# A decoder layer on one core: the expert bias matmul reads 128 rows instead of 24

## The reference, cut to what matters

```python
x = _layernorm(x + _L0_attn_ref(x, ...))             # 16 heads of 8, one shared k and v head
x = _layernorm(x + _L0_xattn_ref(x, ctx_512, ...))   # causal self part plus cross part on 512 rows
x = _layernorm(x + _L0_ffn_ref(x, Wg, W1, b1, Wo, bo))

def _L0_ffn_ref(x, Wg, W1, b1, Wo, bo):              # D = 128, H = 256, E = 8, top 2
    gate_scores = softmax(einsum('btd,ed->bte', x, Wg))
    topk_val, topk_idx = top_k(gate_scores, 2)
    comb = (one_hot(topk_idx, E) * (topk_val / (topk_val.sum(-1) + EPS))[..., None]).sum(-2)
    out = zeros_like(x)
    for e in range(E):
        h = einsum('btd,hd->bth', x, W1[e]) + b1[e]
        a, b = split(h, 2, axis=-1)
        g = a * sigmoid(b)
        eo = einsum('bth,dh->btd', g, Wo) + bo
        out = out + eo * comb[..., e:e + 1]
    return out
```

## Time and profile before

| | |
|---|---|
| median of 3 runs | 259.3 us (259.08 to 259.61) |
| the profiled execution, its own time | 258.73 us |
| its span, first to last instruction | 256.9 us |
| busy, share of the span: TensorE, VectorE, ScalarE, POOL | 76%, 67%, 36%, 23% |
[...]
| F steps: 32 x L601 (64 instructions), 32 x L602 | 39.1 us and 32 x 0.385 us or more |

### The profile page before, as it was taken

The page is one execution under the profiler, slowest core; times in us unless marked ns, Lnnn a source line. Parts: engine busy times, 40 slices in busy tenths (PEclk is TensorE's granted clock), DMA queues, the critical chain, the costliest instruction groups (busy, mean ns, idle before and its releaser), DMA issues.

```text
span 256.9 us, 3649 instructions
## 1 busy us (share of the span) xinstructions
PE 195.1 (76%) x1272; PEld 89.9 (35%) x1280; DVE 172.0 (67%) x423; ACT 91.6 (36%) x138; POOL 58.0 (23%) x85
## 2 busy tenths in 40 slices
PE   3617609988750843788599989999999979999951
PEld 2401103322340531544243435665554322232321
DVE  4719998864560896298988988874317766567742
ACT  4600006578300010343183856568652221222210
POOL 6299995002450176000000000010000100001111
PEclk9955557999995795699999999999999985899975
DMA  6961894000266459620202000000000000000000
GB/s 152 183 71 16 101 104 47 4 2 0 32 55 59 43 73 117 81 87 3 84 0 86 0 1 4 3 2 6 0 3 0 0 4 0 0 0 11 10 0 20
DMA packets 9125, 9.41 MB, mean 37 GB/s; under 512 B 1492, under 2 KB 7052, under 8 KB 9108
## 3 DMA queue, kind: packets, MB, share of 16 engines
q1 hardware_dynamic: 7668, 6.82, 16.3%
q0 software_dynamic: 1440, 2.37, 8.4%
HBM read 4.02 MB, written 0.26 MB: 17 GB/s over the span
## 4 chain that ended last, share of the span: by engine, by line
PE 54%; DVE 19%; DMA 16%; SPq 4%; issue 3%; ACT 2%; POOL 0%; POOLq 0%; another core or an unknown queue 0%; ACTq 0%; DVEq 0%
PE y L528 12%; DVE mneg L695 12%; PE w L601 7%; PE t L601 7%; DMA q_stack_A<-mrow 4%; DMA k_stack_b<-part_k 4%; SPq L378 4%; PE t L497 4%; PE w L452 3%; DMA q_stack_A<-part_q 3%; DMA q_stack_B<-mrow 3%; PE t L479 2%; PE t L486 2%; PE t L602 2%; PE w L602 2%
## 5 line engine op out<-in xcount | busy, mean ns | idle before, releaser
L695 DVE TENSOR_REDUCE mneg<-w 128x1 f32<-128x512 f32 (+2 forms) x128 | 78.1, 651 | 29.3 <-PE w L450 10.0
L887 ACT ACTIVATE probs<-t 128x1024 f32<-128x1024 f32 x48 | 48.4, 1023 | 52.9 <-PE t L479 30.7
L1000 POOL TENSOR_SCALAR rstd<-mv 128x2 f32<-128x2 f32 (+1 forms) x8 | 1.8, 225 | 169.2 <-DVE mv L645 169.2
L452 PE MATMUL w<-k_stack_c,q_stack_A 128*128 128x512 bf16 x56 | 21.2, 390 | 4.6 <-DVE mneg L695 4.0
L442 PE MATMUL w<-k_stack_a,q_stack_A 128*128 128x256 bf16 x64 | 16.1, 360 | 9.6 <-DMA q_stack_A<-part_q 6.8
L884 ACT ACTIVATE probs<-t 128x768 f32<-128x768 f32 x16 | 12.8, 811 | 21.4 <-PE t L491 21.4
L497 PE MATMUL t<-q_stack_A,k_stack_c 128*128 128x256 bf16 x128 | 19.3, 273 | 1.0 <-DVE mneg L695 0.4
L601 PE MATMUL w<-w1T,xT 128*128 128x512 f32 x32 | 19.6, 698 | 0.0
L601 PE MATMUL t<-w1T,xT 128*128 128x512 f32 x32 | 19.5, 694 | 0.0
L528 PE MATMUL y<-probs,v_c 128*32 128x256 f32 x256 | 19.0, 389 | 0.4 <-issue 0.2
L445 PE MATMUL w<-k_stack_b,q_stack_B 128*128 128x128 bf16 x32 | 7.7, 239 | 11.2 <-DMA k_stack_b<-part_k 7.8
(11 more groups left out here) (168 smaller groups left out, 334.3 us busy)
## 6 DMA issues: line engine op xcount, KB each, us to landing
w1T<-in_w1T SPq DMA_DIRECT2D x8, 256.0 KB, 3.1
k_stack_c<-y_sb POOLq DMA_DIRECT2D x6, 256.0 KB, 11.7
rest<-in_rest SPq DMA_DIRECT2D x1, 772.0 KB, 9.7
q_stack_A<-part_q SPq DMA_DIRECT2D x12, 64.0 KB
q_stack_B<-part_q SPq DMA_DIRECT2D x12, 64.0 KB
bias_row<-in_rows SPq DMA_DIRECT2D x1, 384.0 KB, 6.3
k_stack_b<-part_k POOLq DMA_DIRECT2D x6, 64.0 KB, 6.4
k_stack_b<-part_k SPq DMA_DIRECT2D x6, 64.0 KB
```

The costliest lines, as they stand in the source:

```text
L452: last = nc.tensor.matmul(o[:], q[:, head, q0 + qt * P:q0 + (qt + 1) * P], k_stack_c[:, head, b * TC:(b + 1) * TC], start=True, stop=True)
L695: emptied(V.tensor_reduce(out=dst, in_=src, axis=AX.X, op=ALU.max, negate=True), s)
L887: ins = A.activation(dst, o[:], ACT.Exp)
```

## The change

`bias_sel` and `b1_stack` get 128 partitions. Rows 24 to 127 of both are zero, so the product is the same. `b1_stack` is cleared on POOL first, and SP waits for that before the three transfers into rows 0 to 23. The affine selects work on rows 0 to 23 as before. L602 itself reads the same, but its operands now have 128 rows.

```diff
-        bias_sel = sb("bias_sel", [3 * E, E, P], BF16)
+        bias_sel = sb("bias_sel", [P, E, P], BF16)
...
-        b1_stack = sb("b1_stack", [3 * E, 2 * HF], BF16)
+        b1_stack = sb("b1_stack", [P, 2 * HF], BF16)
...
-            "qA0", "qA1", "qB", "qC0", "qC1", "kA", "kB", "kC", "vA", "vB", "vC")}
+            "qA0", "qA1", "qB", "qC0", "qC1", "kA", "kB", "kC", "vA", "b1", "vB", "vC")}
...
             G.memset(half_neg[:], -0.5)
+            G.memset(words(b1_stack[:]), 0.0).then_inc(cleared["b1"], 1)
             for e in range(E):
...
-            link(G.memset(bias_sel[:], 0.0))
+            link(G.memset(words(bias_sel[:].rearrange("p e n -> p (e n)")), 0.0))
             for r in range(3):
-                ins = G.affine_select(out=bias_sel[:], in_=bias_sel[:], compare_op=ALU.not_equal, fill=1.0,
+                ins = G.affine_select(out=bias_sel[0:3 * E], in_=bias_sel[0:3 * E], compare_op=ALU.not_equal, fill=1.0,
...
                         sp.wait_ge(s_parts["b1"], 3)
+                        sp.wait_ge(cleared["b1"], 1)
                         for r in range(3):
```

## The result

The changed kernel takes 250.64 us (median of 6 runs, 249.08 to 252.16), the kernel before on the same chip 259.01 us (6 runs, 256.78 to 259.61). The profiled execution is at the median, 250.64 us, with a span of 248.8. All ratios compare only the executions within 1.5% of the fastest of each kernel, while the medians are over all; in the last group of experiments one early execution of the kernel before (254.56 us) puts the ratios nearer to 1 than the medians, and there I go by medians and traces.

The account below looks back on a forecast made before the run. TensorE bounds the kernel's end, at half clock from 209.6 to 219.8 us. Gains of 3.1 and 0.5 less 0.1 made 3.5 us, so 255.8 us against the 259.3 median; range 253.4 to 257.6, including no fall.

Parts of the forecast that it names:

- Item 4: Bias matmul L602: 128 rows take 389 ns against 385 for 24, over 32 matmuls 0.1 us lost; at most 3.1.
- The slower rival: Between L601 and L602: the 128-row load is no longer hidden; 262.4 us if rows don't affect the clock; chance 0.06.
- Item 1: Low stretch from 209.6 us: with full rows the clock rises at 213.0 instead of 219.8; 3.1 us gained.
- the prediction's own rival: Clock falls neither at 209.6 nor at 247: 4.7 us of low stretch and 1.0 at the end, 253.7 us; chance 0.08.
- The hold from 122 to 126 us: TensorE worked only 1.59 of 4 us, on 128-row matmuls, yet the clock stayed up; taken as evidence that rows count.
- the case for rows: TensorE's clock counts working rows: thin work holds it less than full work; argued from 11.6 and 122 to 126 us.
- Item 2: Behind the gate: VectorE needs 0.9 us an expert against TensorE's 1.37, so it isn't the next bound; cost nothing.
- the sign that VectorE bounds: Between 213 and 219 us: VectorE's wait for TensorE gone while TensorE waits for tiles; would show the forecast wrong.
- Item 3: First of the last two output projections: padding holds the clock high, 0.71 us in place of 1.20; 0.5 us gained.
- Items 5 and 6: POOL's added memset (0.2 us) and larger clear (0.4), and SP's new wait before three b1 transfers: cost nothing.

Follow-up runs that it names:

- the last group of experiments: The 24-row kernel with six unused matmuls at the gate (255.78 us), the changed kernel again (250.33) and versions beyond it, against the kernel before (258.77).
- the one kernel with 24 rows that was kept high: Changed kernel with L602 reading 24 rows, plus six unused 128-row matmuls filling TensorE's wait at the gate of batch 1; 255.78 us against 258.77 before.

## Why the prediction was wrong

The sign was right, the size was not: 3.5 us were forecast, 8.4 came. By the steps of the prediction:

- **Item 4, the padded matmul itself, is the step that failed.** It gave 0.1 us lost where the runs show 5.4 us gained, and it closed the range on the other side with "From below nothing: no less work is issued". Less work isn't issued, but less waiting is: 0.29 us a step, the largest term. I compared durations (385 and 389 ns), and matmuls overlap: in the trace of after, L601 starts 0.22 us behind the start of a bias matmul of 0.38 us (216.92 and 217.14). What counts is the distance from start to start. The earlier trace rows held the step, 1.37 us. What it should have been the trace of after shows: 0.22 us from L602 to L601 for the 512 columns of one matmul, 0.86 from L601 to L602, four times as much, 1.08 in all.
- **The slower rival had the place right and the sign wrong.** It supposed that a 24-row load slips in beside the running matmul and a full one doesn't. The loads of after and of 65 rows show the reverse: they start 0.42 or 0.43 us ahead, that of 24 rows with its matmul (222.71 and 222.72).
- **Item 1, the clock.** 3.1 us were put on a rise at 213.0. Where the clock fell with full rows it rose at 213.2 and 213.3; in four other traces with 65 rows or more it didn't fall at the gate. By medians the clock is worth 3.0 us, but that is for no fall at all, which the prediction's own rival priced at 4.7, and 3.1 was for a fall of 3.4 us: that the two sizes agree is in part luck. The reason isn't shown as I gave it. With 24-row experts behind the gate there are two low stretches of 10.2 us (before, 24 rows) and two of 3.4 us, one of the latter with all bias matmuls thin. No trace with full rows has a long one; they are not the only thing that goes with a short one. The hold from 122 to 126 us, on which the case for rows rested, doesn't bear it either: in 11 of the 14 traces the clock does fall there, at 125.5 to 127.9 us, also behind 128-row matmuls. And L419 wasn't the one other thin matmul, since L459 reads 64 rows too.
- **Item 2, VectorE.** I cost it at nothing for steps of 1.37 us. At 1.08 against its 0.9 it is too near: TensorE waits 0.59, 0.86 and 2.77 us for it behind the gate, the first of these between 213 and 219, which the prediction had named as the sign that VectorE bounds. 22 experts with 0.29 us each are 6.4 us; of the 9.5 us gained in that stretch some 4.7 are the clock's, so 4.8 of them arrived.
- **Item 3, the end.** The first of the last projections took 0.93 us, between the two values; it started after a gap of 2.77 us, and the clock fell during it, at 240.2. Of 0.5 us, 0.3 came, and the longer wait for VectorE took more: the stretch behind the last expert is 0.4 us longer than before, and 1.2 longer than in both traces with 24 rows and the new memsets (11.6).
- **Items 5 and 6** held in that they cost nothing. The memset of b1_stack took 0.30 us (0.2 forecast), that of the selector 0.52 (0.4), and SP's b1 transfers were issued at 78.94 against 78.55; the run with 24 rows has all of it and the time of before:

```profile
30.08 0.30 POOL L980 MEMSET b_stack<- 128x256 f32 x1
...
38.09 0.52 POOL L988 MEMSET bias_sel<- 128x512 f32 x1
...
61.90 0.24 POOL L1001 TENSOR_SCALAR rstd<-mv 128x2 f32<-128x2 f32 x1 [19.61 <-DVE mv L645]
```

The sum from the last group of runs: 3.0 us for the clock and 5.4 us for the bubbles, 8.4 us. It is that between the medians of the first comparison too, which confirms the whole and not how it splits: the split rests on the one kernel with 24 rows that was kept high.

## What to carry to other kernels

Where a matmul on few rows stands between full ones, read the distance from start to start, not the duration, and set it against that of full matmuls with as many columns: here the surplus was load time that isn't hidden, 0.29 us a step. Reading 65, 96 or 128 rows, the added ones zeros, took it away at the price of a memset of 0.30 us, and putting thin matmuls of 24 rows side by side took half of it without (2.45 us for two experts in place of 2.74). Then look at the next engine first: here VectorE, at 0.9 us an expert, took a quarter of what the padding gave behind the gate, and of 32 x 0.29 = 9.3 us in the whole kernel 5.4 arrived.

## What was not expected of the hardware

- The bubble is all or nothing: 1.37 us a step with 24 and with 64 rows, 1.08 with 65, 96 and 128. It stands at a change between thin and full: 24 rows behind 24 have none, with 0.23 us from start to start and the load 0.22 us ahead.
- A matmul of 128 rows mostly zero isn't slower than one of 24: 379 ns against 385.
- The clock differs between executions of one kernel in the same places: the first expert starts between 183.7 and 187.2 us over all traces, in no order of rows, and the same kernel had a low stretch of 3.4 us at the gate once and none the other time. A change of a microsecond in this kernel needs more than one trace.
